# Splitting the vector engine's routing of a group of sequences into two stages of its hand-written order

## The reference, cut to what matters

```python
x = x + attn(layernorm(x))                    # 16 heads, causal, rotary factor
x = x + cross_attn(ctx, ctx, layernorm(x))    # 1 head over 128 keys
h = layernorm(x)
probs = softmax(h @ router_w.T)               # 8 experts
rw, sel = top_k(probs, 2)
moe = sum over the two chosen experts of rw * (silu(h @ w_gate[e]) * (h @ w_up[e])) @ w_down[e]
shared = silu(h @ sw_gate) * (h @ sw_up) @ sw_down
out = x + moe + sigmoid(h @ gate_w.T) * shared
```

## Time and profile before

| | |
|---|---|
| median of 3 runs | 529.49 us (528.92 to 531.44) |
| the profiled execution | 527.34 us, of which the span of the trace is 525.6 us |
| busy in the span | PE 85%, DVE 67%, ACT 56%, PEld 58%, POOL 38% |
| mean granted clock of PE | 0.942 |

### The profile page before, as it was taken

One profiled execution on the slowest core, in us unless ns is written; L12 is line 12 of the kernel. 1 busy time (PEld: TensorE's weight loads), 2 busy tenths in 40 slices (PEclk: granted clock), 3 DMA queues, 4 the chain that ended last, 5 costly groups with the idle time before them and its releaser, 6 DMA issues.

```text
span 525.6 us, 13729 instructions
## 1 busy us (share of the span) xinstructions
PE 446.2 (85%) x4508; PEld 303.0 (58%) x4508; DVE 354.0 (67%) x1236; ACT 295.0 (56%) x951; POOL 201.1 (38%) x247
## 2 busy tenths in 40 slices
PE   4758999998979979979989988577899989989993
PEld 3324555655545535545555555356677777777783
DVE  4564667778758758757777675885566666656585
ACT  1126777878757758757777856641444544434430
POOL 8602030022153153152213325653255555555572
PEclk9969999999989999988999989769899999989998
DMA  7600001001010010020111012512322222221194
GB/s 199 161 12 14 32 3 52 10 32 38 19 67 23 18 67 23 19 68 17 34 58 34 18 44 81 175 47 62 78 83 80 76 79 81 77 78 57 44 345 132
DMA packets 41604, 34.69 MB, mean 66 GB/s; under 512 B 6464, under 2 KB 36432, under 8 KB 41536
## 3 DMA queue, kind: packets, MB, share of 16 engines
q1 hardware_dynamic: 36478, 24.51, 16.2%
q0 software_dynamic: 4320, 8.99, 5.1%
q10 hardware_dynamic: 738, 0.33, 0.2%
HBM read 17.26 MB, written 12.09 MB: 56 GB/s over the span
## 4 chain that ended last, share of the span: by engine, by line
PE 64%; DVE 14%; ACT 8%; issue 7%; another core or an unknown queue 4%; POOL 1%; DMA 0%; SPq 0%; ACTq 0%; DVEq 0%; POOLq 0%
PE ps_scores L855 7%; PE ps_shared L723 6%; PE ps_scores L677 6%; ACT probs L949 5%; PE ps_scores L706 5%; PE ps_shared L863 4%; PE ps_shared L872 4%; PE ps_scores L809 4%; PE ps_shared L660 3%; PE ps_scores L702 3%; PE ps_shared L773 2%; PE ps_scores L847 2%; PE ps_scores L711 2%; PE ps_scores L684 2%
## 5 line engine op out<-in xcount | busy, mean ns | idle before, releaser
L610 POOL DMA_INDIRECT ys<-ctx_t,xload x71 | 69.0, 972 | 66.7 <-ACT ctx_t L1044 50.3
L949 ACT ACTIVATE probs<-ps_scores 128x512 f32<-128x512 f32 x128 | 73.4, 612 | 14.8 <-PE ps_scores L711 14.8
L597 POOL TENSOR_TENSOR x1b<-x,bias 128x128 f32<-128x128 f32 x32 | 14.6, 456 | 159.7 <-DVE x L1178 159.6
L591 POOL DMA_INDIRECT xs<-xrow,posu x64 | 64.2, 1003 | 27.4 <-DVE rsum L1279 13.8
L855 PE MATMUL ps_scores<-wide,xe 128*128 x213 | 69.2, 435 | 1.1 <-DVE xe L1351 1.1
L945 ACT ACTIVATE s_copy<-ps_scores 128x512 f32<-128x512 f32 x64 | 37.5, 598 | 38.4 <-PE ps_scores L684 30.3
L1157 DVE TENSOR_REDUCE negmax<-ps_scores 128x4 f32<-128x512 f32 x64 | 42.8, 676 | 19.7 <-PE ps_scores L684 17.3
L1362 DVE COPY probs<-ps_shared 128x256 f32<-128x256 f32 x71 | 30.1, 424 | 33.9 <-PE ps_shared L863 19.2
L1034 ACT ACTIVATE xe<-ps_scores 128x128 fp32r<-128x128 f32 x71 | 19.8, 278 | 50.3 <-PE ps_scores L847 38.5
L872 PE MATMUL ps_shared<-wd,probs 128*128 x284 | 44.2, 279 | 0.1
L677 PE MATMUL ps_scores<-wide,qk 32*128 32x512 f32 x256 | 38.0, 664 | 6.7 <-ACT probs L949 4.4
(11 more groups left out here) (219 smaller groups left out, 1034.2 us busy)
## 6 DMA issues: line engine op xcount, KB each, us to landing
xload<-xs SPq DMA_DIRECT2D x71, 66.0 KB
wide<-qk SPq DMA_DIRECT2D x64, 64.0 KB, 1.9
wide<-ys SPq DMA_DIRECT2D x8, 512.0 KB, 8.6
ctx_t<-in_ctx SPq DMA_DIRECT2D x32, 64.0 KB, 2.0
out_x<-res SPq DMA_DIRECT2D x8, 256.0 KB, 3.1
ys<-ctx_t,xload POOLq DMA_INDIRECT x71
wd<-in_L_ffn_w_down SPq DMA_DIRECT2D x8, 128.0 KB, 3.4
xs<-xrow,posu POOLq DMA_INDIRECT x64
```

The lines of the kernel that those rows point to most:

```text
L591: pool.indirect_dma_start(out=xs, out_offset=bass.IndirectOffsetOnAxis(ap=posu[:, g % 2, k, u:u + 1], axis=0), in_=xrow[:, g % 2, k, u, :] ...
L610: pool.indirect_dma_start(out=ys, out_offset=bass.IndirectOffsetOnAxis(ap=xload_i[:, i % XL, C + 1:C + 2], axis=0), in_=ybuf[:, i % 4, :], ...
L949: act.activation(probs[:, b % 2, j * HJ:(j + 1) * HJ, :].rearrange("p a t -> p (a t)"), SC[score_bank(("scores_t", b), j)][:], ACT.Exp)\
```

## The change

The DVE stage `route` becomes two. Its first half is now called `choose` and stands one slot earlier (ahead -10 in place of -11), behind `norm_ffn`. Its second half keeps the name `route` and its slot, and now stands behind `norm_ffn` and `norm_x_stats`, directly ahead of `ranks`. Nothing that is computed changes, and the lists of the other engines are untouched. `choose` is also added to the stages that get a group's number and to the table of DVE's stages. In the changed file a line number is larger by one up to `choose`, and by three from `route`'s second half on (L1255 becomes L1258).

```diff
     "DVE": [
         ("xscores", -5, None, None),
         ("weights", -36, None, None),
-        ("route", -11, None, 0),
         ("row_max", 0, 3, None),
         ("router", -7, None, None),
         ("attn_out", -3, None, None),
         ("turn_xprobs", -5, None, None),
         ("tall_sums", -2, None, None),
         ("norm_ffn", -6, None, None),
+        ("choose", -10, None, 0),
         ("norm_x_stats", 8, None, 0),
+        ("route", -11, None, 0),
         ("ranks", -11, None, 0),
...
-            def route(g):
+            def choose(g):
                 p = g % 2
                 w.bank_read(("router", GB * (g + 1) - 1))
                 m8, i8 = mx8[:, p], ix8[:, p]
...
                 ins.then_inc(ranked, 1)
 
+            def route(g):
+                p = g % 2
                 for u in range(GB):
                     w.ge(scattered[p][u], 16 * 2 * (g // 2))
                 dve.tensor_copy(xrow[:, p, 1, :, 0:C], xrow[:, p, 0, :, 0:C])
```

More of the change, by code:

```diff
@@ L141 @@
 LATE = {"weights": NJ, "split": 2, "gate_up": 1}
-GROUP_STAGES = ("norm_x_stats", "rstd_x", "norm_x", "turn_x", "project", "route", "ranks")
+GROUP_STAGES = ("norm_x_stats", "rstd_x", "norm_x", "turn_x", "project", "choose", "route", "ranks")
 ENTRIES = [entry for entries in ORDER.values() for entry in entries]
@@ L1333, in _ @@
             w.run("DVE", dict(norm_x_stats=norm_x_stats, turn_x=turn_x, project=project, row_max=row_max, tall_sums=tall_sums, attn_out=attn_out, norm_xattn=norm_xattn, norm_ffn=norm_ffn, xscores=xscores,
-                       turn_xprobs=turn_xprobs, xout=xout, router=router, route=route, ranks=ranks, weights=weights, split=split))
+                       turn_xprobs=turn_xprobs, xout=xout, router=router, choose=choose, route=route, ranks=ranks, weights=weights, split=split))
             dve.wait_ge(wgu_split, E)
```

## The result

The changed kernel took 533.67 us (median of 20 runs, 529.86 to 567.78), the kernel before beside it 531.24 us (20 runs, 527.89 to 534.65). The run of 567.78 us had a granted clock of 0.733 and is left out of the ratio. That ratio is 1.0037 with a 95% interval of 1.0020 to 1.0054: **slower by 2.0 us (1.1 to 2.9)**. The forecast was +0.75 us and 530.2 us, its range ended at 533.0.

What follows compares the result with a forecast made beforehand. DVE was taken to be late in the routing's slot, with PE waiting for it; the terms -0.01 + 0.33 + 0.49 + 0.49 - 0.12 - 0.43 + 0 + 0 = +0.75 us put 529.49 at 530.2 us, range 527.3 to 533.0.

Steps and rivals of the forecast that it cites:

- The whole head start is eaten: Group 0, routing's slot: MAX8 starts 1.29 us earlier, but L1211 comes at 124.15 against 124.16; -0.01 us.
- issue: What the profile's row names as ending L737's wait; the prediction took DVE's L1211, ending 0.06 us before, instead.
- Rival A: PE keeps its gain: L790's waits go, 3.4 us together, and L737 doesn't wait for L1211; 526.1 us, chance 0.12.
- Groups 1 to 3, the second half: Routing's slot: the second half, hidden before behind late L784, counts in full; +0.33, +0.49 and +0.49 us.
- Rival B: Groups 1 to 3: PE's longer wait before L737 halves its clock; 532.8 us for one group, 538 for three; chance 0.22.
- `choose` vanishes in that: Groups 1 to 3, slot before the routing's: `choose` fits in the 3.12 us idle before L1211, costing nothing.
- the whole sum: All groups' terms added: +0.75 us, 0.14%.
- the place that I called covered: Group 5, slot before the routing's: `choose` has the same cover as group 4, where L1211 waits 0.22 us for L773.
- Groups 6 and 7: Both taken as 0; group 6 bounded by -0.4 to +0.5 us, group 7 covered by DVE's 1.05 us wait before `ranks`.
- rival C: Group 5: without L790's wait PE's clock stays up, 2.6 us less; 527.6 us, chance 0.10.
- the band that was called no change: Whole kernel: differences within about 0.5% (2.65 us) count as no change; chance of the same 0.64.

Runs made afterwards that it cites:

- `choose` alone: Kernel before with only `choose` one slot earlier, second half left ahead of `row_max` part 3: 482.36 us (0.9849) at 490 us, 528.47 us (0.9938) at 530 us.
- second execution: The changed kernel, nothing altered, profiled again in the first batch at 530 us: 532.13 us, a single run.
- second half alone: Kernel before with `choose` where all of `route` was, second half directly ahead of `ranks`: 490.60 us (1.0007) at 490 us, 529.32 us (1.0017) at 530 us.
- `choose` alone with the edit on POOL: Kernel before with only `choose` one slot earlier, and POOL's `norm_x` behind `scatter` part 1: 515.69 us, ratio 0.9750, in the last batch.

## Why the prediction was right, and where it was too small

**The mechanism held.** "The whole head start is eaten" is what group 0 shows at both levels, and `choose` alone shows its other side: with the second half elsewhere the head start is kept, 1.34 us in group 0 at 490 us. L1211 was what L737 waits for, not "issue": in the changed kernel the row itself names it (0.42 us for L1212). Rival A is out: of all that PE got ahead of L738, both slots of group 0 together kept 0.04 us and those of group 4 0.05 us (8.30 + 9.33 before, 8.37 + 9.21 after), where 0.12 was forecast; in the second execution group 4 even lost 0.26 us.

**Groups 1 to 3, the second half.** Forecast +0.33, +0.49 and +0.49; with 3.4 us at half clock in both kernels r1 has +0.38 us, and the second half alone, with 3.4 us as well, +0.40 (10.85 us). There the term was sized right. In r3, with 6.8 us, it is +0.44 in the changed kernel and -0.31 with the second half alone (11.42 us): in five slots of these orders with 6.8 us it is 11.42 to 12.17 us, so what the term is worth there stays open. The second half alone came to +0.9 us (-0.8 to +2.6) at 530 us, sum +1.3, and this interval holds zero as well. At 490 us, where there is no late L784 to hide behind, it changed nothing, since nothing is lost that was hidden.

**Rival B, the clock,** had a time, 532.8 us, that is the nearest of all to the measured one, and from the first profile I would have taken it for the cause. That nearness is chance. PE's wait ahead of L737 in the slots of the routing was to grow from 0.92 to 1.25 us or more. In groups 1 to 3 it is 0.42 us in both executions; with the wait ahead of L780 it makes 0.88, 1.05 and 1.26 us in the first. No stretch at half clock follows it in any of them. What is longer is the half clock behind the stall, and not always: a second execution of the same kernel has a short one in groups 1 and 3. A longer one as a rule would lower the mean granted clock, by an estimated 0.006 (half of 6.8 us in 530) for 3.4 us more in two groups, of which 0.003 come back behind group 5 (below). The median of that mean is 0.943 over the changed kernel's 19 runs in the ratio and 0.942 over the kernel before's 19 and 17 runs of the last two batches (the record has no clocks of the 20 beside it). That speaks against a lasting effect, weakly: one stretch of 3.4 us more, 1.2 to 1.3 us of time, isn't excluded. Through the last L1212 of the first part that second execution stands 1.18 us behind the kernel before (266.53 against 265.35 us from first to last L1211), the first one 3.93 us. What moves the length from execution to execution is open. The Trainium skill, "TensorE: Matmul & The Clock Gate", section "HAM oscillation — how this bites in real kernels", says that idle gaps of the matrix engine bring its half clock back. The stalls of 3.12 us do here, and where they are absent, at 490 us, there is none between groups 0 and 4. Between the two it isn't clean: in the last batch PE's clock stayed up behind DVE's waits of 1.1 to 1.8 us in group 1, and fell for 3.4 us behind one of 1.16 us in group 3 (`choose` alone with the edit on POOL). By its picture a longer wait ahead of L737 could have been paid for again; in these runs no half clock follows that wait.

**The step that failed: "`choose` vanishes in that".** I gave `choose` nothing in the slots of the stall and in that of group 5. In the two executions at 530 us it costs 0.04 and 0.17 us in c1, 0.13 and 0.09 in c2, 0.16 and 0.19 in c3, and 0.47 us in group 5 in both. That is no variation between executions: `choose` alone has +0.16, +0.10, +0.19 and +0.47 us in the same slots, and the second half alone, without `choose` there, is within 0.01 us of the kernel before in all four. It makes 0.8 to 0.9 us, as much as the whole sum, and with it the sum would be +1.6 us, inside the measured 1.1 to 2.9. Two more terms that I had at nothing, group 6's +0.25 and the slot behind group 5 with -0.9 (both below), take it to about +0.95 us, so part of the 2.0 us stays unexplained. I had taken a stall without a known cause as a place in which work is free. It hides most of `choose`, and `choose` meets POOL in there and grows itself by 0.6 us; that this growth is what gets through is argued, not shown. In group 5 the place that I called covered ends in a signal that arrives late (at 490 us `choose` costs 0.13 us there). PE and DVE in time, the changed kernel:

```profile
307.14 0.42 PE L685 MATMUL ps_scores<-causal,ident 32*32 32x512 bf16 x16
```

```profile
308.31 0.69 DVE L1158 TENSOR_REDUCE negmax<-ps_scores 128x4 f32<-128x512 f32 x1 [0.49 <-PE ps_scores L685]
```

1.17 us lie between the two starts; in the kernel before, one slot without `choose`, it was 302.35 to 302.80, 0.45 us. With the gain of 0.40 us in the slot after it (forecast 0.43), group 5 came to +0.07.

**What the rows can't close.** Behind the last L1211 (L1212), where of the change only group 7's routing still stands, the profiled executions at 530 us take between 184.5 and 190.5 us to their end, those at 490 us 166.8 to 168.7. So a single execution can't carry a difference of 2 us in the whole, and 1 us of it can't be given to a slot.

**Groups 6 and 7, and rival C.** In group 6 `choose` costs 0.98 us in its own slot and the next gives back 0.73, +0.25 us where I took 0, inside the bound of -0.4 to +0.5. The slot right behind group 5's routing, before these, is the one that I overlooked. The kernel before, and the changed kernel in its first execution:

```profile
310.80:317.60 6.80, 6.33 (x52) 3.88 (x52) 2.95 (x14) 2.76 (x12) 1.58 (x2) 0.51 0.17 50
```

```profile
317.90:321.30 3.40, 3.40 (x45) 2.28 (x44) 0.99 (x4) 1.85 (x7) 0.35 (x1) 0.52 0.11 34
```

6.8 us at half clock against 3.4, and the slot takes 8.82 us against 7.95. This goes with the order of DVE's list: at 530 us the kernel before has 6.8 us there with POOL's old list and with its edited one (8.82 and 8.83 us), the changed kernel 3.4 in all three executions (7.95, 7.84 and 7.84), `choose` alone none in three of four (6.33). At 490 us the kernel before has 3.4 us (7.77) and the changed kernel none (6.34). That is rival C's direction and, at 0.9 to 1.0 us, a third of its price, and it is more than the whole of the 0.6 to 0.75 us that the changed kernel gains from there to the end of the first part at 530 us (at 490 us 1.4 of 1.9). It is few executions, so the rule is likely and not proved, and that L790's lost wait is what does it was not tested.

**The range** failed by 0.67 us, and for its centre more than its width: it stood on three runs with a median of 529.49, and 20 gave 531.24. Moved up by these 1.75 us it would have held 533.67. The ratio, 1.0037, lies inside the band that was called no change.

## What to carry to other kernels

When an early start is bought for one instruction, follow it to the next instruction that another engine waits for; here the second half, put between the two, gave back 1.18 of 1.34 us, and ahead of the first it cost nothing. Ask of every idle stretch which instruction ends it and why, before work is priced at nothing in it: here the idle time of 3.12 us was the larger prize (8.4 us at 530 us for moving one line on POOL) and not quite a free place. And before a mechanism is built on one pair of traces, profile the same kernel a second time.

## What the runs showed that was not expected

- **At one of two levels signals between engines are late while indirect DMAs run.** The same kernel takes 490 us in two batches and 528 to 531 in the others; of the 37.3 us between two profiled executions 17.6 lie up to the last L1211 and 19.7 behind it. Where it takes 530, the signal that PE's L684 gives to DVE and ACT is late by the same amount for both, in a slot of group 0 with two scatters (L591 at 129.48 and 130.78 us). DVE and ACT in time, at 530 us:

```profile
132.29 0.69 DVE L1157 TENSOR_REDUCE negmax<-ps_scores 128x4 f32<-128x512 f32 x1 [0.75 <-PE ps_scores L684]
```

```profile
132.41 0.60 ACT L945 ACTIVATE s_copy<-ps_scores 128x512 f32<-128x512 f32 x1 [0.99 <-PE ps_scores L684]
```

  and at 490 us, where DVE's instruction has no wait:

```profile
132.24 0.60 ACT L945 ACTIVATE s_copy<-ps_scores 128x512 f32<-128x512 f32 x1 [0.23 <-PE ps_scores L684]
```

  ACT's wait is 0.76 us longer. At 530 us L1211 (L1212) waits 1.1 to 1.8 us in groups 1 to 3 with three scatters in a row beside it, 2.5 to 3.1 with four and 2.7 to 4.5 with five (three orders of POOL's list); at 490 us it has no wait with the same four. That the wait goes with the scatters is shown in both directions by the runs that moved them. SP's copies (L467) run beside all these stalls at 530 us, though not beside the late signal of group 0 above, so whether they have a share in the length is open. So is by what path a scatter delays another engine's signal, and what sets the level.
- **DVE and POOL slow each other in small instructions with two inputs:** one addition of 0.16 us took 0.44 beside L598, a pair of comparisons 0.56 in place of 0.28. The Trainium skill, "SBUF — State Buffer", section "Who interferes with whom", says that a DVE instruction with two inputs in SBUF contends with a GpSimd one that reads SBUF, and the third addition, which ends 0.04 us after L598, agrees. The first addition's 0.47 us, beside a scatter alone, is not explained by these runs: with the edits on POOL the additions ran beside a scatter as well, and the four took their usual 0.75 us.
- **The half clock behind one and the same stall is 3.4 us long in one execution and 6.8 in another,** and costs 1.2 to 1.3 us a time in the changed kernel. The second half alone has a third length, 10.2 us in group 2 (193.4 to 203.6 us, granted clock 0.51), in a slot of 12.46 us.
